# Normalisation roots as full-width rows on ScalarE: one variance matmul per chunk in place of columns, GpSimd powers and spread transposes

## What is computed

```python
x = x + attn_a(layernorm(x))      # cosine attention in a window, 16 heads of 8
x = x + ffn0(layernorm(x))        # silu(x wg) * (x wu), then wd; hidden 384
x = x + attn_b(layernorm(x))      # sigmoid gate, tanh, linear scan, + its own input
x = x + ffn0(layernorm(x))
x = x + attn_c(layernorm(x))      # softmax attention with a decay, low-rank keys and values
x = x + ffn1(layernorm(x))
...
```

## Time and profile before

| | |
|---|---|
| median of three runs | 1240.3 us (1234.19 to 1241.84) |
| the profiled execution | 1232.48 us, its span 1230.7 us |
| busy in the span | TensorE 1085.4, VectorE 779.7, ScalarE 593.0, GpSimd 213.9 us |
| granted TensorE clock over the span | 0.936 of full speed |

### The profile page before, as it was taken

How to read it: one execution, slowest core, us unless ns; L and a number is a source line. 1 busy time by engine, 2 the same in 40 slices (tenths; PEclk the granted TensorE clock), 3 DMA queues, 4 the chain that set the end, 5 groups by cost and what they waited for, 6 DMA issues and landing times. The chain is left out here.

```text
span 1230.7 us, 15242 instructions
## 1 busy us (share of the span) xinstructions
PE 1085.4 (88%) x5700; PEld 446.8 (36%) x5700; DVE 779.7 (63%) x1250; ACT 593.0 (48%) x1030; POOL 213.9 (17%) x125
## 2 busy tenths in 40 slices
PE   6799998984898888888888989999799858899998
PEld 3233554341222332333333334444343413344443
DVE  3677347367999899899896213015499888893200
ACT  3686222243057777777776763223853174311311
POOL 1111732034000000000000000001064323451000
PEclk8899998996579999999999999999899768899999
DMA  7000000034210110101000000000000000000000
GB/s 246 1 1 1 1 1 1 0 118 162 95 53 32 68 45 30 56 26 38 7 4 7 4 5 1 0 1 1 0 1 1 0 0 1 1 1 0 18 1 17
DMA packets 20767, 32.02 MB, mean 26 GB/s; under 512 B 6748, under 2 KB 14940, under 8 KB 20312
## 3 DMA queue, kind: packets, MB, share of 16 engines
q1 hardware_dynamic: 20696, 31.07, 7.4%
HBM read 23.23 MB, written 7.57 MB: 25 GB/s over the span
## 5 line engine op out<-in xcount | busy, mean ns | idle before, releaser
L976 DVE CUSTOM_DVE_ANT_0 SQ<-PS,XP 128x1024 bf16<-128x1024 f32 x256 | 303.5, 1219 | 36.0 <-PE PS L966 36.0
L1088 ACT ACTIVATE arena<-PS 128x384 f32<-128x384 f32 (+1 forms) x512 | 252.1, 551 | 146.5 <-PE PS L1063 145.8
L966 PE MATMUL PS<-arena 48*128 48x512 bf16 (+3 forms) x704 | 201.3, 356 | 20.1 <-DMA arena<-scr 12.7
L1063 PE MATMUL PS<-arena 50*128 50x512 bf16 (+3 forms) x640 | 152.2, 321 | 19.0 <-ACT arena L1088 11.3
L1079 PE MATMUL PS<-arena 128*32 128x512 f32 (+1 forms) x1280 | 137.4, 518 | 19.5 <-ACT arena L1094 18.7
L1495 PE MATMUL PS<-arena,w_h1T 128*128 128x512 f32 x256 | 117.5, 605 | 14.2 <-ACT arena L1523 7.3
L1523 ACT ACTIVATE arena<-PS,w_scl 128x512 f32<-128x512 f32 x64 | 43.7, 687 | 173.0 <-PE PS L1495 172.9
L1495 PE MATMUL PS<-arena,w_h2T 128*128 128x512 f32 x256 | 115.1, 595 | 0.0
L1063 PEld LDWEIGHTS PS<-arena 50*128 50x128 bf16 x640 | 42.6, 94 | 146.4 <-ACT arena L1088 139.4
L1540 DVE SCALAR_TENSOR_TENSOR XR<-PS,w_scl,XR 128x512 f32<-128x512 f32 x8 | 6.0, 750 | 130.3 <-PE PS L1504 130.3
L1717 DVE TENSOR_TENSOR_SCAN arena<-arena 128x512 f32<-128x512 f32 x64 | 83.5, 1304 | 0.1
(11 more groups left out here) (225 smaller groups left out, 1627.5 us busy)
## 6 DMA issues: line engine op xcount, KB each, us to landing
scr<-arena SPq DMA_DIRECT2D x16, 384.0 KB, 3.0
arena<-scr SPq DMA_DIRECT2D x64, 96.0 KB
arena<-scr SPq DMA_DIRECT2D x64, 64.0 KB
arena<-scr SPq DMA_DIRECT2D x64, 32.0 KB
XP<-xT SPq DMA_DIRECT2D x1, 1024.0 KB, 4.8
w_h1T<-h1T SPq DMA_DIRECT2D x1, 1024.0 KB, 6.6
w_h2T<-h2T SPq DMA_DIRECT2D x1, 1024.0 KB, 8.7
out_xT<-XR SPq DMA_DIRECT2D x4, 256.0 KB, 2.2
```

The lines of the kernel that those rows point to most:

```text
L966: mm = t.matmul(PS[:, bank, k0 - lo:k1 - lo], packed(m, g, v, slice(q * P, (q + 1) * P), KP), packed(m, g, 2 + v, slice(k0, k1), KP), star ...
L976: v.tensor_tensor_reduce(JUNK[:, u % 2, :], PS[:, bank:bank + 2, :].rearrange("p a b -> p (a b)"), STRIP[:, at:at + S], 1.0, -3.0e38, ALU. ...
L1063: mm = t.matmul(PS[:, score_bank(T, i), at:at + b_ - a_], packed(n, g, 2 + v, slice(kt * P, (kt + 1) * P), KP + MROWS), packed(n, g, v, sl ...
L1088: nc.scalar.activation(PT[:, T % 2, score_head(T, i), a0_:a1_], PS[:, score_bank(T, i), a0_:a1_], ACT.Exp).then_inc(s_free, 1)
```

## The change

Norms 0 to 4: VectorE's copy, the column matmuls, the addition of eps, the power and the transposes go. The stationary operand is now a full matrix of 1/128 and the moving one SQ, so that one float32 matmul per chunk gives the variance of every token on all partitions, in two PSUM banks used in turn (`VAR_BANKS`). ScalarE takes the logarithm of variance plus eps and then the exponential of -1/2 times it, in the order Ln 0, Ln 1, Exp 0, Exp 1, Ln 2, Ln 3, Exp 2, Exp 3. VectorE multiplies the centred chunk in PSUM by it into XN. Stages behind a norm that use the variance banks wait for its last logarithm. Tables are loaded by hand: the logarithm's at the start of each norm, silu's ahead of each F0 loop. In A0 the sums of squares of chunk 0 go ahead of the value matmuls. A1's first VectorE step waits for the whole norm, and GpSimd's fills of constants for A1 no longer stand behind the powers.

The last group of A1: one matmul with a 0/1 matrix gives every row its denominator, ScalarE takes the logarithm and the exponential of its negative into SQ, VectorE multiplies.

The removed bodies of `ln_pe`, `ln_act`, `ln_pool`, `ln_dve`, `sums_pe` and `spread_sums_pe` are shown above and are left out here; so are the renumbering of counts in the late norms and edits of names.

```diff
     c["groupmean"] = same(P // 8) / 16
+    spread = np.zeros((P, P), f)
-        for a in range(NG):
-            pick[32 * g + HD, a, :, a, g] = 1
-    c["pick"] = pick.reshape(P, NG * 32)
+        spread[32 * g + HD, 32 * g:32 * g + 32] = 1
+    c["denspread"] = spread
     c["ident"] = np.eye(P, dtype=f)
...
+        LN_BANKS = ((4, 5, 6, 7), (4, 5, 7, 6), (6, 7, 5, 4), (4, 5, 6, 7), (6, 7, 5, 4))
+        VAR_BANKS = ((2, 3), (1, 3), (2, 3), (1, 3), (2, 3))
+        LOG_EXP = "natural_log_exp_and_others"
...
+        def ln_pe(t, k, stage):
+            src = XP if stage < 2 else XR
             for c, bank in enumerate(LN_BANKS[k]):
...
+                if c >= 2:
+                    t.wait_ge(ln_log, NCH * k + c - 1)
+                t.matmul(PS[:, VAR_BANKS[k][c % 2], :], mean[:], SQ[:, c, :], start=True, stop=True).then_inc(ln_var, 1)
+        def ln_act(a, k):
+            nc.scalar.preload_act_table_set(LOG_EXP)
             for c, bank in enumerate(LN_BANKS[k]):
                 a.wait_ge(ln_centered, NCH * k + c + 1)
                 nc.scalar.activation(SQ[:, c, :], PS[:, bank, :], ACT.Square).then_inc(ln_squared, 1)
+            for c0 in (0, 2):
+                for c in (c0, c0 + 1):
+                    a.wait_ge(ln_var, NCH * k + c + 1)
+                    nc.scalar.activation(SQ[:, c, :], PS[:, VAR_BANKS[k][c % 2], :], ACT.Ln, bias=eps[:, 2:3]
+                                         ).then_inc(ln_log, 1)
+                for c in (c0, c0 + 1):
+                    a.wait_ge(ln_log, NCH * k + c + 1)
+                    nc.scalar.activation(SQ[:, c, :], SQ[:, c, :], ACT.Exp, scale=-0.5).then_inc(ln_root, 1)
+        def ln_dve(v, k):
             for c, bank in enumerate(LN_BANKS[k]):
+                v.wait_ge(ln_root, NCH * k + c + 1)
+                v.tensor_tensor(XN[:, c * CH:(c + 1) * CH], PS[:, bank, :], SQ[:, c, :], ALU.mult).then_inc(ln_free, 1)
...
         def a0_v_pe(t, c, part):
+            if c == 0:
+                t.wait_ge(ln_log, NCH)
...
         def a0_pe(t):
             a0_qk_pe(t, 0)
+            a0_ss_pe(t, 0)
             a0_v_pe(t, 0, 0)
             a0_v_pe(t, 0, 1)
-            a0_ss_pe(t, 0)
...
                     r = (NJ0 * j + b) % 2
                     t.wait_ge(f0_h_free, m + 1)
+                    if j == 0 and b == 1:
+                        t.wait_ge(ln_log, NCH * (k + 1))
                     t.matmul(PS[:, 2 + r, :], ffn0[:, HID0 + b * P:HID0 + (b + 1) * P], x, start=True,
...
                     nc.scalar.activation(F0_SG[:, r, :], PS[:, r, :], ACT.Silu).then_inc(f0_silu, 1)
+            nc.scalar.preload_act_table(ACT.Silu)
             pairs(a, body)
...
                 if c < NCH:
                     t.wait_ge(ln_free, ln_count(k, c if c < 2 else NCH - 1))
+                    if c == 1:
+                        t.wait_ge(ln_log, NCH * (k + 1))
...
                 t.wait_ge(a1_kv, c + 1)
+                if c == 0:
+                    t.wait_ge(ln_log, NCH * 5)
...
         def a1_prep_dve(v):
             v.wait_ge(a1_tab, 48)
+            v.wait_ge(ln_free, ln_count(4, NCH - 1))
...
             g.wait_ge(x_ready, 1 + NCH)
-            g.wait_ge(ln_inverse, 2 * 2)
+            g.wait_ge(a0_qz, GH * NCH)
...
         def a1_prep_pool(g):
-            g.wait_ge(ln_inverse, 2 * 5)
             with g.Fori(0, NCH // 2) as i:
...
             if c == 2:
                 t.wait_ge(ln_free, 1 + late_count(LN5[0], 1))
             t.wait_ge(o_free, 2 * NGRP + c - 3)
-            sums_pe(t, A1_SUM[c], lambda a: output(c, LAST), a1_sum)
-        def last_spread_pe(t, c):
-            t.wait_ge(a1_rs, c - 1)
-            spread_sums_pe(t, A1_SPREAD[c], LAST, RSUM[:, 0, :], a1_bc)
-        def last_inverse_dve(v, c):
-            v.wait_ge(a1_sum, c - 1)
-            v.reciprocal(RSUM[:, 0, :], PS[:, A1_SUM[c], 0:P]).then_inc(a1_rs, 1)
+            t.matmul(PS[:, A1_SUM[c], :], denspread[:], output(c, LAST), start=True, stop=True).then_inc(a1_sum, 1)
+        def last_inverse_act(a, c):
+            if c == 2:
+                a.wait_ge(p1_free, NUNIT)
+            a.wait_ge(a1_sum, c - 1)
+            nc.scalar.activation(SQ[:, c, :], PS[:, A1_SUM[c], :], ACT.Ln).then_inc(a1_rs, 1)
+            a.wait_ge(a1_rs, c - 1)
+            nc.scalar.activation(SQ[:, c, :], SQ[:, c, :], ACT.Exp, scale=-1.0).then_inc(a1_bc, 1)
         def last_norm_dve(v, c):
             v.wait_ge(a1_bc, c - 1)
-            v.tensor_tensor(output(c, LAST), output(c, LAST), PS[:, A1_SPREAD[c], :], ALU.mult).then_inc(a1_inv, 1)
+            v.tensor_tensor(output(c, LAST), output(c, LAST), SQ[:, c, :], ALU.mult).then_inc(a1_inv, 1)
...
                 if T == LAST_SUMS:
                     last_sums_pe(t, 2)
-                if T == LAST_SPREAD:
-                    last_spread_pe(t, 2)
             last_sums_pe(t, 3)
             project_pe(t, 3, 0)
             project_pe(t, 3, 1)
-            last_spread_pe(t, 3)
             project_pe(t, 3, 2)
             project_pe(t, 3, LAST)
...
                     half_out(a, n - 1, 1)
                 if is_diag(T):
                     diag_exp_act(a, T)
+                if T == LAST_SUMS:
+                    last_inverse_act(a, 2)
             half_out(a, NGRP - 1, 1)
+            last_inverse_act(a, 3)
...
-                if T == LAST_SUMS + 1:
-                    last_inverse_dve(v, 2)
-                if T == LAST_SPREAD + 1:
+                if T == LAST_SUMS + 2:
                     last_norm_dve(v, 2)
             a1_residual_dve(v, 2)
-            last_inverse_dve(v, 3)
             last_norm_dve(v, 3)
...
         @block.scalar
         def _(a):
-            nc.scalar.preload_act_table_set("natural_log_exp_and_others")
+            a.wait_ge(consts_ready, 5)
             wait_loads(a, 0)
             ln_act(a, 0)
             wait_loads(a, 1)
...
         @block.gpsimd
         def _(g):
             g.wait_ge(consts_ready, 1)
-            for k in range(5):
-                ln_pool(g, k)
-                if k == 0:
-                    a0_pool(g)
-                if k == 1:
-                    a1_minus_ones(g)
-                if k == 3:
-                    g.wait_ge(ln_inverse, 2 * 4)
-                    a1_ones(g)
+            a0_pool(g)
+            a1_minus_ones(g)
+            g.wait_ge(x_ready, 1 + NCH * 3)
+            a1_ones(g)
             a1_pool(g)
             late_pool(g)
```

More of the change, by code:

```diff
@@ L166, in build @@
         groupmean, statecol = load("groupmean", P), load("statecol", (DS // 4) * 32)
-        negrow, pick = load("negrow", P), load("pick", NG * 32)
+        negrow, denspread = load("negrow", P), load("denspread", P)
         tri = load("tri", 2 * DS)
@@ L226, in build @@
         NW = CH // P
-        LN_BANKS = {k: (4, 5, 6, 7) for k in (0, 3, 7, 8)}
-        LN_BANKS[1] = (4, 5, 7, 6)
-        LN_BANKS.update({2: (6, 7, 5, 4), 4: (6, 7, 5, 4), 5: (6, 7, 4, 5), 6: (2, 3, 6, 7)})
+        LN_BANKS = ((4, 5, 6, 7), (4, 5, 7, 6), (6, 7, 5, 4), (4, 5, 6, 7), (6, 7, 5, 4))
+        VAR_BANKS = ((2, 3), (1, 3), (2, 3), (1, 3), (2, 3))
+        LOG_EXP = "natural_log_exp_and_others"
         ln_centered, ln_squared, ln_copied, ln_var = sem("ln_centered"), sem("ln_squared"), sem("ln_copied"), sem("ln_var")
+        ln_log, ln_root = sem("ln_log"), sem("ln_root")
         ln_moved, ln_inverse, ln_spread = sem("ln_moved"), sem("ln_inverse"), sem("ln_spread")
@@ L242, in ln_count @@
             return 1 + NCH * k + c + 1
-        def ln_at(bank):
-            return NW * (bank % 2)
-        def ln_pe(t, k, stage, src=None):
-            src = src if src is not None else XP if stage < 2 else XR
+        def ln_pe(t, k, stage):
+            src = XP if stage < 2 else XR
             for c, bank in enumerate(LN_BANKS[k]):
-                if src is XN:
-                    t.wait_ge(ln_free, ln_count(k - 1, c))
-                elif stage > 0:
+                if stage > 0:
                     t.wait_ge(x_ready, 2 + NCH * (stage - 1) + (c // 2 * 2 + 1 if stage == 2 else c))
@@ L257, in ln_pe @@
                          stop=True).then_inc(ln_centered, 1)
-            for c, bank in enumerate(LN_BANKS[k]):
+            for c in range(NCH):
                 t.wait_ge(ln_squared, NCH * k + c + 1)
-                t.wait_ge(ln_copied, NCH * k + c + 1)
-                for w in range(NW):
-                    mm = t.matmul(PS[:, bank, w:w + 1], SQ[:, c, w * P:(w + 1) * P], mean[:, 0:1],
-                                  start=True, stop=True, skip_group_check=True)
-                mm.then_inc(ln_var, 1)
-            for c, bank in enumerate(LN_BANKS[k]):
-                t.wait_ge(ln_inverse, 2 * k + c // 2 + 1)
-                for w in range(NW):
-                    at = ln_at(bank) + w
-                    mm = spread_column(t, PS[:, bank, w * P:(w + 1) * P], VAR[:, 1, c // 2, at:at + 1])
-                mm.then_inc(ln_spread, 1)
-        def ln_act(a, k, dst=None):
+                if c >= 2:
```

(24 more changed lines are left out.)

44 lines of the change are left out of this document (7 added, 37 removed).

## The result

The changed kernel takes 1219.02 us (median of 4 runs, 1218.07 to 1220.34) beside 1238.45 for the kernel before (4 runs, 1234.19 to 1241.84): a ratio of 0.985, interval 0.981 to 0.988. Times are medians; ratios and intervals are of the means. One execution of the kernel before, of 2063.76 us, stands apart from all others and is left out of every comparison.

What follows compares the result with a forecast made beforehand. The kernel was taken as a chain of stages, each norm costing the time from its variance matmuls to the next stage's critical step. Savings of 2.5 + 1.4 + 2.6 + 1.4 + 3.0 + 1.65 = 12.55 gave 1227.7 us, range 1221 to 1236.

Steps and rivals of the forecast that it cites:

- norm 0 into A0: From norm 0 to A0's chain L491: 2.5 us saved, the middle between 1.6 at half clock and 3.5 at full.
- norm 1 into F0: From norm 1 to F0's first silu: silu starts 7.95 us behind the first variance record instead of 9.38, 1.4 saved.
- norm 2 into B0: From norm 2 to B0's first tanh: it starts at 182.18 instead of 184.81, 2.6 us saved.
- norm 3 into F0: From norm 3 to F0: the same pattern as norm 1, 1.4 us saved.
- norm 4 into A1: From norm 4 to A1's first VectorE step: it starts at 255.13 instead of 258.20, 3.0 us saved.
- end of A1, last chunk and chunk 2: A1's last group: F1 starts 1.45 us sooner through the last chunk, plus 0.2 from chunk 2, bounds -1.2 and +1.3.
- The pitch on ScalarE: In each norm, ScalarE's eight Ln and Exp follow with 0.02 to 0.04 us between two, Exp 3 ending at 6.63.
- The 3.5: Norm 0 into A0 at the full clock: L491 starts at 22.4 instead of 25.92, 3.5 us saved.
- The loop's loads: Rival, chance 0.14: a load stays inside F0's loop, costing 2.6 us in norms 1 and 3; gain 10.0, 1230.3.
- a switch costs its row: Opposing rival, chance 0.05: three table switches in norms 1 to 3 cost twice their row; gain 8.7, 1231.6.
- the best ends: Rival, chance 0.13: full clock in A0's beginning and all of TensorE's share in A1's chunk 2; gain 14.7, 1225.6.
- The slower case: Rival, chance 0.06: A1's half clock lasts longer, 0.95 us per pair of steps; with 40 pairs 1266.

Runs made afterwards that it cites:

- typical execution: The kernel before run once more with no edit, its profiled execution taking 1237.39 us; its 12 runs had a median of 1238.71 us.
- third run of the changed kernel: The changed kernel repeated with no edit, against the kernel before on the same chip: 1217.38 us beside 1240.32, ratio 0.983.
- alternated order: The changed kernel with each chunk's Exp directly behind its Ln in the norms: 1218.56 us, the changed kernel beside it 1217.38.
- pair of kernels with extra matmuls: The changed kernel with, behind every norm's variance matmuls, four full float32 matmuls (1230.29 us) or 32 records of one column (1239.57 us).

## Why the prediction was wrong where it was

The mechanism was right: the gain comes out of the five norms and the end of A1, each stage giving its part. Two steps of the sum failed: the distance between two activations, and the places of the consumers taken from one profile of before, with the clock that this one had. In one table, in us; the second column against the one profile of before, the third the typical execution of before (span 1235.6) against the third run of the changed kernel (span 1214.7), in which the last row closes the sum:

| term | predicted | against the profile of before | typical execution |
|---|---|---|---|
| norm 0 into A0 | 2.5 | 2.87 | 1.67 |
| norm 1 into F0 | 1.4 | 2.24 | 2.89 |
| norm 2 into B0 | 2.6 | 3.43 | 5.45 |
| norm 3 into F0 | 1.4 | 2.38 | 2.84 |
| norm 4 into A1 | 3.0 | 3.44 | 5.37 |
| end of A1, last chunk and chunk 2 | 1.65 | 1.5 | 1.5 |
| all else | 0 | -2.4 | 1.2 |
| sum | 12.55 | 13.5 | 20.9 |

Norms 1 to 4 alone: 8.4 predicted, 11.5 against the profile of before (3.1 more, by the pitch on ScalarE), 16.55 in the typical execution (5.05 more of clock).

**The pitch on ScalarE ("0.02 to 0.04 between two"): wrong.** Neighbours that don't depend on each other lie over each other by about 0.11. Over the norm, with six such pairs, it is 0.8: silu at 7.14 instead of 7.95, and the same 0.8 in norm 2. The alternated order shows that it is the dependence which decides. I had added up single durations, most out of rows in which the activation had a wait in front of it. The overlap stood in my own rows: in the earlier trace rows two activations with a bias column take 1.27 together, where two of 0.69 would make 1.38. I read that row for the table load alone.

**Norm 4, VectorE's first step at 7.41: it starts at 7.04.** The products end at 6.64, but now A1's first matmuls are last (VectorE waits 0.41 for them in the third run of the changed kernel), so only 0.4 of the 0.8 comes through. The table of A1 wasn't late. The gain against the profile of before was 3.44, close to the 3.0.

**The clock taken as the profile of before had it: wrong, and the largest error.** In norm 0 I saw the low clock and took half of it into the sum; in the four other norms I took the consumer's place from one profile as it stood. In the typical execution these four are 5.05 longer (46.43 against 41.38): 3.95 of it in norms 2 and 4, where the half clock lasts twice as long, and 1.1 in norms 1 and 3, where it comes later. After the change they are the same in every profile, so this goes too. The pair of kernels with extra matmuls shows that the columns can do it: 0.95 us of work more, 9.3 us of time, 7.3 of it seen in the norms of the profile. In the one profile of the kernel before filled up with full matmuls, the clock stays up through norms 2, 3 and 4. I had the hint in my hand and wrote it off: the profiled execution of before was 0.6% below the median of its runs. I took the same microseconds off the median, as if what made the others longer couldn't lie in the part that goes. It did, for the most part, in the longer execution of before that was profiled (and in that with the end of A1 alone changed, which has the same four norms); those of 1240 us and more, at a mean clock of 0.927 to 0.928, have no profile, and where they lose the rest stays open. That is why the range, which was made of ScalarE's prices and of the spread of the median, ended at 1221.

**Norm 0: the size fair, the reason wrong.** The chain started at 23.05, 23.15 and 23.30 in the three profiles of the changed kernel, inside the 22.4 to 24.3. Measured from the first variance record the norm is 4.2 shorter in the first of them than in the profile of before; but that record comes 1.4 later there (12.94), and at 11.65 and 11.86 in the two others. The 3.5 was ascribed to the sums' place ahead of the value matmuls, and that place is worth nothing: the sums wait for VectorE's evictions, and it is these that come earlier. That the sums might meet the half clock was right in two of three profiles (3.36 and 3.29 us instead of 1.96). The reason given for it, column matmuls and waits, doesn't hold there, since no column matmul is left; the change takes the low clock out of norms 1 to 4 and not out of this one.

**The end of A1: right.** 1.45 predicted for the last chunk, 1.4 measured. F1 stands 4.39 behind the last denominators' matmul, 4.3 predicted. Chunk 2's stretch, from its exponentials to the last copy, went from 20.72 to 20.64: 0.1 of the 0.2, and neither of its bounds came near.

**The rivals.** The loop's loads went, and a switch costs its row: 1.28 and 0.01 to the next activation, on the path. By the Trainium skill (ScalarE: Activation LUTs, What ACT_TABLE_LOAD costs) there would be 1.38 more; the trace doesn't agree. Of the best ends, the full clock in A0's beginning came in one profile of three, and chunk 2's share didn't come. The slower case did not come about as told. Its stage was well chosen, though: the walk was 436.0 to 442.1 us in the profiles without added matmuls in it, and about the longer, the more of it lies at the half clock: 436.0 with 56.5 us, 437.5 with 61.8, 439.7 with 66.4, 442.1 with 75.7. The half clock around its start lasts 64.9 to 78.5 us, most of it ahead of the 345 us at which the earlier trace rows begin, and TensorE isn't idle in it, here in the first profile of the changed kernel:

```profile
285.00:325.00 40.00, 35.10 (x95) 8.20 (x95) 39.93 (x72) 0.00 (x0) 0.00 (x0) 0.50 0.36 128
```

The 3.6 that this profile lost against that of before isn't from there, as its stretch at the start was of the shortest (64.9 against 68.3), but from the second one, of 10.2 us near the walk's end. "The same within 2 us" was too narrow. It isn't tied to the change, as the repeats of both kernels at 436.0 to 437.0 show, but what sets these stretches in an execution stays open.

**The baseline.** 1240.3 was the median of three runs; the repeats gave 1237.5 to 1240.3. Up to 2.8 us of the miss in the time, though none of that in the gain, may be this.

## What to carry to other kernels

Matmuls of one column can cost more than their records: the clock can fall in or behind them while the engine looks busy, and the next stage's full matmuls pay. Where a change takes such a stretch away, take profiles of two executions of different length, or give a part of the difference between the profiled execution and the median to the stretch, and let the range reach to it. For a row of activations, ask of every neighbouring pair whether the second needs the first.

## What the runs showed of the hardware

- The granted clock was 0.66 and then 0.57 in the mean of 5 and 4 us beside a TensorE that was busy for 9.00 of 9.00 us by its records, within a run of one-column float32 matmuls and just behind it. In another norm of the same profile it stayed at 1.00 beside the same run.
- It was 0.50 for 40 us on end, around A1's start, beside a TensorE busy for 35.10 of them.
- Executions of one kernel whose mean clock is the same, 0.936, differ by 5 us (1232.48 and 1237.39), as it matters in which stage the low clock lies. The changed kernel had its 4 to 6 runs within 2.1 to 3.1 us on a chip, the kernel before its 4 to 23 runs within 7.7 to 11.3 us.
- Activations of 512 columns overlap by 0.10 to 0.12 us if the second needs nothing of the first, and have a gap of 0.03 if it does. A table load of 1.28 us had no time hidden behind it.
